# Column copies by byte offset, seven batches per chunk on ScalarE, in halves of 16

## The chip, the cores and the metric

The kernel runs on one core of a Trainium2 chip. The metric is the device time of one execution in microseconds (us). An edge-softmax graph layer is computed in float32; nothing but the time changes with the edit described here.

## The reference

There are 12,500 nodes with 64 features, and 200,000 edges sorted by their target node, each with a source node, a target node and 64 edge features. `h` is the layer-normed and rectified `x`. Then, with two heads:

```
h_edge = ((h[src] + edge_attr) @ W)          # E x 2 heads x 64
s      = leaky(h_edge . attn_l + (h @ W . attn_r)[dst], 0.2)
alpha  = softmax of s over the edges of one target node
ft     = segment_sum(h_edge * alpha, dst);  y = mean over the two heads
out    = x + relu(batchnorm(y))
```

The kernel never forms `h_edge`. It sums `(h[src] + edge_attr) * weight` per node first and multiplies by `W` at the end.

## The kernel before, in words

**Chunks and tiles.** The edges are cut into 49 chunks (`NCH`), a chunk into 16 groups of 256 edges (`CG`, `GROUP`), and a group into two tiles of 128 edges (`EPP`). So a chunk has 32 tiles. Every tile needs the 128 rows `h[src]` of its edges. They come in three ways:

- by default as an indirect DMA of GpSimd, one for each tile (`gather`, line 691, issued on line 698), from the table `h_tab` in DRAM;
- one tile in some chunks (five of eight chunks from chunk 6 on) as 128 small DMAs of SyncE, one for each row (`load_rows`, line 572, `row_tiles`, line 83). The offset of each row is read from the tile `offs` into a register, sixteen at a time (line 459). These offsets are already in bytes;
- the column tiles (`col_tiles`, line 65) as copies inside the on-chip memory. `acc` holds the transposed table (`hT_cols`) in its partitions 96 to 127, and one instruction copies the column of one edge (32 partitions x 2 elements, the two halves of the 64 features) into the buffer `cols`. The column number comes from the tile `coffs` into a register (`col_regs`, line 466). Group 12 is the one treated so: both its tiles in a chunk from chunk 5 on, but only one tile in the chunks whose number leaves 1 when divided by 4 (5, 9, ... 45), and one in the last chunk.

**Who copies the columns.** The 128 columns of a tile are four batches of 32. Batches are dealt in rounds of seven (`COL_BATCHES = (6, 1)`): ScalarE copies six (`load_cols`, line 832), VectorE the seventh (line 1456). The round that is dealt in chunk c starts from batch 7 x (c - 3), so it runs about two chunks ahead of the use. For a batch, an engine reads 32 registers in one load (line 468), then for each column does one fused register instruction that works out the address, and one copy. TensorE adds the copied columns into the transposed edge features (`turn(c, 3)`, line 959) and into the scores (`col_scores`, line 989, which increments `cols_read`); `cols` has room for four tiles.

**The order on ScalarE in a chunk** (`chunk`, line 844):

```
act.wait_ge(open_diff, c + 1)
nc.scalar.activation(fexp[:, :], fdif[:, :], ACT.Exp)      # line 854
act.wait_ge(diff_ok, c + 1)
nc.scalar.activation(pT[:, :], sdif[:, :], ACT.Exp)        # line 858
z_keep_halves(b)                                           # line 829
load_cols(c)                                               # line 863
```

So the two waits of the softmax lie next to each other, and all copies come behind them, before the first wait of the next chunk. VectorE makes `fdif` and, a little later, `sdif` (line 1518). TensorE turns `pT` (line 1064) and increments `p_turned`; VectorE then makes the weighted one-hot tile `scaled`, TensorE forms the sums, VectorE adds them to `acc`.

**What ties GpSimd to the rest** (`keep_step_late`, line 681): from chunk 5 on, the second gather of chunk c waits for the sums of chunk c - 2, and the eighteenth for the turned exponentials of chunk c - 1. Each gather of a buffer also waits until the same buffer has been used two chunks before (`e_ok`).

**Preparation.** `coffs` is worked out once by ten VectorE instructions (lines 1408 to 1417) from `src`, before the first chunk; ScalarE waits for it (`coffs_ok`).

Of the kernel before, what the change touches and what calls it, by code (L numbers as in the profile page):

```python
# [4 lines left out]
N, E, F, H = 12500, 200000, 64, 2  # L5
P = 128
EPP = 2
# [10 lines left out]
NCH = -(-E // CHUNK)  # L18
# [13 lines left out]
NACC = N + WIN  # L32
# [24 lines left out]
COL_G = 12  # L57
COL_FIRST = 5
COL_BUFS = 4
COL_BATCH = 32  # L60
COL_BATCHES = (6, 1)
COL_ROUND = sum(COL_BATCHES)


def col_tiles(c):

    if c < COL_FIRST:
        return []
    return [(j, COL_G) for j in range(1 if c % 4 == 1 or c == NCH - 1 else EPP)]


def cols_upto(c):

    return sum(len(col_tiles(i)) for i in range(c + 1))


def col_batches_upto(c):

    n = cols_upto(c) * P // COL_BATCH
    return n - n // COL_ROUND, n // COL_ROUND  # L80


def row_tiles(c):
# [30 lines left out]
def gnn_kernel(nc, x, src, dst, ea, w_l, gb_l, src_l, src_q, src_c, dst_l, dst_pad, dst_n, dst_r, base_l, base_q, base_o, ea_t, out):  # L114
    f32, i32, u8 = mybir.dt.float32, mybir.dt.int32, mybir.dt.uint8
    ALU, ACT, AX = mybir.AluOpType, mybir.ActivationFunctionType, mybir.AxisListType

    def view(ap, dims, off=0):

        return bass.AP(ap.tensor, ap.offset + off, [list(ap.ap[0])] + [list(d) for d in dims])  # L120

    with ExitStack() as ctx:
        def sb(name, shape, dt=f32):
            return ctx.enter_context(nc.sbuf_tensor(name, shape, dt))
# [11 lines left out]
        acc = sb("acc", [P, H, NACC])  # L136
        accf = acc[:, :, :].rearrange("p h n -> p (h n)")
# [11 lines left out]
        HALF = F // H  # L149
        CP = P - HALF  # L150
# [15 lines left out]
        coffs, coffs_t, coffs_u = (sb(n, [P, EPP * P], i32) for n in ("coffs", "coffs_t", "coffs_u"))  # L166
        row_tile = sb("row_tile", [P, ROW_BUFS, FH])
        cols = sb("cols", [P, COL_BUFS, H, P])
# [37 lines left out]
        cc = sb("cc", [R2, 2, R2])  # L206
# [244 lines left out]
        def tiles_of(c, k):  # L451

            return [(j, g) for g in range(k * GQ, (k + 1) * GQ) for j in range(EPP)
                    if (c * CG + g) * GROUP + j * P < E
                    and (j, g) not in row_tiles(c) + col_tiles(c)]

        def far_regs(c, o0, o1):
# [3 lines left out]
                skip_runtime_bounds_check_because="src and dst hold numbers of nodes")[1]  # L461

        col_batches = [(c, j, r0) for c in range(NCH) for j, g in col_tiles(c) for r0 in range(0, P, COL_BATCH)]
        assert len(col_batches) <= COL_ROUND * (NCH - COL_FIRST)

        def col_regs(c, o0, o1, which):

            return nc.values_load_multi_w_load_instructions(  # L468
                coffs[c:c + 1, o0:o1], engines=[which], min_val=0, max_val=N - 1,
                skip_runtime_bounds_check_because="src and dst hold numbers of nodes")[1]  # L470

        h_bytes = h_tab.rearrange("n f -> (n f)").bitcast(u8)
# [21 lines left out]
        def z_seen(c):  # L494

            return list(range(z_upto(c - 2), z_upto(c - 1)))


        HT = [(i, min(i + 4, NB // EPP)) for i in range(0, NB // EPP, 4)]

        HT_OF = [[n for n, (i, _) in enumerate(HT) if b0 <= i * EPP < b1] for b0, b1 in QS]
        assert all(EPP * HT[n][1] <= b1 for ns, (_, b1) in zip(HT_OF, QS) for n in ns)

        def hT(n):
# [7 lines left out]
        ENG = mybir.EngineType  # L512
# [6 lines left out]
        def _(sp):  # L519
# [72 lines left out]
            for c in range(1, NCH):  # L592
# [6 lines left out]
                if c >= ROW_FIRST - 1:  # L599
                    sp.wait_ge(p_turned, c)  # L600
                    load_rows(c, 1)

            sp.wait_ge(cols_ok, col_batches_upto(NCH - 1)[0])
            sp.wait_ge(cols_dve_ok, col_batches_upto(NCH - 1)[1])
            sp.wait_ge(zT_ok, Z_IN)
            sp.dma_start(zT[F:P, 0:Z_IN, :], view(acc[0:F, 1, :], [[NP_, Z_IN], [1, NP_]])).then_inc(z_packed, 16)
# [22 lines left out]
            for i, (b0, b1) in enumerate(OUT):  # L629
                sp.wait_ge(y_ok, 1 + [t1 for _, t1 in TURN].index(b1))  # L630
                sp.dma_start(y_rows[0:PS[1], b0:b1], xres[0:PS[1], b0:b1]).then_inc(out_in, 16)
# [117 lines left out]
        def _(act):  # L749
# [70 lines left out]
            def z_keep(b, turned, kept):  # L820

                act.wait_ge(turned, b + 1)
                nc.scalar.activation(zT[:, b, :], z_turned(b), ACT.Copy).then_inc(kept, 1)

            def z_keep_halves(b):

                act.wait_ge(zT_made, b + 1)
                for r in range(NR):
                    kept = nc.scalar.activation(acc[0:F, r, b * NP_:(b + 1) * NP_], z_turned(b)[r * F:(r + 1) * F], ACT.Copy)
                kept.then_inc(zT_ok, 1)  # L830

            def load_cols(c):

                b0 = COL_ROUND * (c - COL_FIRST + 2)
                for cc, j, r0 in col_batches[b0:b0 + COL_BATCHES[0]]:
                    n = cols_upto(cc - 1) + j
                    if n >= COL_BUFS:
                        act.wait_ge(cols_read, n - COL_BUFS + 1)
                    for i, r in enumerate(col_regs(cc, j * P + r0, j * P + r0 + COL_BATCH, ENG.Activation), r0):
                        copied = nc.scalar.activation(view(cols[0:HALF, n % COL_BUFS, 0, i:i + 1], [[P, H]]),  # L840
                                                      view(acc[CP:P, 0, bass.ds(r, 1)], [[NACC, H]]), ACT.Copy)
                    copied.then_inc(cols_ok, 1)

            def chunk(c):

                if c == NCH - 1:
                    act.wait_ge(cols_dve_ok, col_batches_upto(c)[1])
                    z_keep(NZ - 5, zT_made, zT_ok)
                if c == NCH - 1:
                    z_keep(NZ - 4, zT_made, zT_ok)  # L850
                act.wait_ge(open_diff, c + 1)
                if c:
                    act.wait_ge(open_all, c)
                nc.scalar.activation(fexp[:, :], fdif[:, :], ACT.Exp).then_inc(open_exp, 1)  # L854
                act.wait_ge(diff_ok, c + 1)
                if c:
                    act.wait_ge(p_turned, c)
                nc.scalar.activation(pT[:, :], sdif[:, :], ACT.Exp).then_inc(p_ok, 1)
                if c < NCH - 1:
                    for b in z_seen(c):  # L860
                        z_keep_halves(b)
                if COL_FIRST - 2 <= c < NCH - 2:
                    load_cols(c)

            def root_table():

# [3 lines left out]
            def closing():  # L870

                chunk(NCH - 1)
                for b in range(NZ - 3, NZ):
                    if b == NZ - 1:
                        root_table()
                        act.wait_ge(last_read, 1)
                    z_keep(b, zT_made, zT_ok)
# [3 lines left out]
            for c in range(NCH - 1):  # L881
                chunk(c)
# [266 lines left out]
        def _(dve):  # L1149
            v = nc.vector  # L1150
            done = [v_steps, 0]

            def step(ins):

                done[1] += 1
                ins.then_inc(done[0], 1)
                dve.wait_ge(done[0], done[1])
# [6 lines left out]
            def signal(s):  # L1164
                dve.sem_inc(s, 1)  # L1165
# [240 lines left out]
            node, t, u = (a[0:NCH, :] for a in (coffs, coffs_t, coffs_u))  # L1406
# [8 lines left out]
            step(v.tensor_scalar(node, node, 1, None, ALU.logical_shift_right))  # L1415
            step(v.scalar_tensor_tensor(t, node, float(NP_), t, ALU.mult, ALU.add))
            step(v.scalar_tensor_tensor(node, u, float(NH), t, ALU.mult, ALU.add))
            signal(coffs_ok)

            def z_block(b, made, read, turned):  # L1420
# [35 lines left out]
            def load_cols(c, i):  # L1456

                if c == COL_FIRST - 2:
                    dve.wait_ge(cols_table_in, 32)
                b0 = COL_ROUND * (c - COL_FIRST + 2) + COL_BATCHES[0] + i  # L1460
                for cc, j, r0 in col_batches[b0:b0 + 1]:
                    n = cols_upto(cc - 1) + j
                    if n >= COL_BUFS:
                        dve.wait_ge(cols_read, n - COL_BUFS + 1)
                    for i, r in enumerate(col_regs(cc, j * P + r0, j * P + r0 + COL_BATCH, ENG.DVE), r0):
                        copied = v.tensor_copy(view(cols[0:HALF, n % COL_BUFS, 0, i:i + 1], [[P, H]]),  # L1466
                                               view(acc[CP:P, 0, bass.ds(r, 1)], [[NACC, H]]))
                    copied.then_inc(cols_dve_ok, 1)

            def chunk(c):  # L1470
# [94 lines left out]
                for i, (g0, g1) in enumerate(sums_of(c)):  # L1565
                    dve.wait_ge(sums_made, 2 * c + i + 1)
                    for g in range(g0, g1):
# [10 lines left out]
                        else:  # L1578
                            added.then_inc(sums_added, 1)
                    if i < COL_BATCHES[1] and COL_FIRST - 2 <= c < NCH - 2:  # L1580
                        load_cols(c, i)
# [165 lines left out]
```

## Time and profile before

| | |
|---|---|
| median of three runs | 3050.21 us (3046.49 to 3059.28) |
| span of the profiled execution, first to last instruction | 1885.4 us |
| the profiled execution's own time beside its span | not given; the median less the span is 1164.8 us |
| POOL (GpSimd) busy | 1389.6 us, 74% |
| DVE (VectorE) busy | 1312.1 us, 70% |
| ACT (ScalarE) busy | 1041.5 us, 55% |
| PE (TensorE) busy | 1042.3 us, 55% |
| DMA engines busy, mean | 83 GB/s moved over the span |

Register, branch and semaphore instructions are not counted as busy, so an engine that mostly loads registers and works out addresses looks idler than it is. An engine's name with a q behind it (ACTq, DVEq, SPq) is its sequencer: the views show register loads (TENSOR_LOAD) and fused register operations (FUSED_REGOPS) under it. "Issue" is time in which an engine waited for nothing that the profile shows. Times in rows are us from the start of the span.

### The profile page before, as it was taken

The numbers are of one execution on the slowest core, as the hardware profiler recorded it, in microseconds if no ns is written. First come the engines' busy times: TensorE is split into PE (matmuls) and PEld (weight loads), VectorE is DVE, ScalarE is ACT, GpSimd is POOL, SyncE is SP. The second block draws the span as 40 slices with busy tenths as digits, with TensorE's granted clock in tenths as the row PEclk, the third lists the DMA queues.
The fourth block names the chain that finished last, engine by engine and source line by source line (L and its number), as shares of the span: only waits on it lengthen the run. The fifth ranks groups of instructions, "written<-read, shape, count | busy, mean of one in ns | idle before, by whom it ended". The sixth has DMA issues, their size and how long they took to land.

```text
span 1885.4 us, 47594 instructions
## 1 busy us (share of the span) xinstructions
PE 1042.3 (55%) x6860; PEld 792.2 (42%) x6860; DVE 1312.1 (70%) x4737; ACT 1041.5 (55%) x8591; POOL 1389.6 (74%) x1477
## 2 busy tenths in 40 slices
PE   2726646556545744655554565545654654564466
PEld 1614534444434533533443353434433543453355
DVE  7878877776676766776766866766766667667676
ACT  2520366666655665666565565665665565566522
POOL 7777677777777777777777777777777777777770
PEclk9857766667666766666666666666666666676667
DMA  8643232232222223222322232232223222222335
GB/s 232 172 107 96 61 89 72 64 95 66 64 84 77 64 64 97 64 64 63 98 64 64 63 98 64 63 97 64 64 63 98 64 63 79 82 64 63 97 72 140
DMA packets 77196, 156.31 MB, mean 83 GB/s; under 512 B 34116, under 2 KB 38736, under 8 KB 70224
## 3 DMA queue, kind: packets, MB, share of 16 engines
q1 hardware_dynamic: 28818, 99.91, 15.9%
q0 software_dynamic: 46944, 49.57, 13.1%
q10 hardware_dynamic: 1112, 3.73, 0.8%
q14 instruction: 266, 2.18, 0.4%
q8 instruction: 56, 0.92, 0.2%
HBM read 141.85 MB, written 9.80 MB: 80 GB/s over the span
## 4 chain that ended last, share of the span: by engine, by line
POOL 59%; issue 21%; PE 7%; DVE 7%; DMA 2%; ACT 2%; ACTq 1%; DVEq 0%; SPq 0%
POOL work L698 58%; PE po L1084 2%; ACT cols L840 1%; PE p_s L985 1%; ACTq L468 1%; PE p_s L947 1%; DMA er_run<-er_tab,er_idx 1%; DMA acc<-in_x 1%; PE pt L972 1%; DMA h_tab<-acc 1%; PE p_s L1014 1%; PE pt L936 1%; DVE work L1215 0%; DVE onehot L1358 0%; POOL er_run L712 0%
## 5 line engine op out<-in xcount | busy, mean ns | idle before, releaser
L698 POOL DMA_INDIRECT work<-h_tab,srcI x1396 | 1319.7, 945 | 430.0 <-issue 423.5
L840 ACT ACTIVATE cols<-acc 32x2 f32 x8352 | 928.3, 201 | 493.8 <-issue 460.6
L1084 PE MATMUL po<-scaled,work 128*65 128x64 f32 x3104 | 297.4, 284 | 60.5 <-issue 57.5
L1084 PEld LDWEIGHTS po<-scaled,work 128*65 128x65 f32 x3104 | 292.0, 200 | 78.0 <-issue 77.1
L1466 DVE COPY cols<-acc 32x2 f32 x1376 | 178.1, 189 | 160.6 <-issue 142.0
L972 PE MATMUL pt<-ident,work 128*128 128x128 f32 x784 | 194.7, 391 | 59.4 <-DVE work L1215 59.3
L1022 PE MATMUL p_s<-ident,elh 128*32 128x128 f32 x196 | 50.6, 411 | 303.9 <-DVE elh L1210 303.9
L1210 DVE COPY elh<-work 128x16 f32<-128x16 f32 (+2 forms) x222 | 40.5, 195 | 227.0 <-DMA work<-h_tab,srcI 225.1
L1570 DVE TENSOR_TENSOR acc<-acc,po 65x64 f32 x776 | 168.4, 217 | 28.0 <-PE po L1084 1.6
L985 PE MATMUL p_s<-work,wpair 128*32 128x256 f32 x784 | 180.5, 384 | 1.6 <-DVEq L1165 1.6
L972 PEld LDWEIGHTS pt<-ident,work 128*128 128x128 f32 x784 | 139.0, 200 | 88.6 <-DVE work L1215 64.2
L1022 PEld LDWEIGHTS p_s<-ident,elh 128*32 128x32 f32 x196 | 25.7, 155 | 315.5 <-DVE elh L1210 311.4
L1061 PE MATMUL p_m<-fexp,ones 1*65 1x2 f32 x98 | 18.4, 255 | 238.5 <-ACT fexp L854 238.5
L1215 DVE TENSOR_TENSOR work<-work,pt 128x512 f32<-128x512 f32 (+2 forms) x222 | 132.7, 607 | 5.9 <-PE pt L972 5.7
L1542 DVE TENSOR_TENSOR scaled<-onehot,p_m 128x2048 f32<-128x2048 f32 x48 | 109.6, 2284 | 19.3 <-PE p_m L1064 18.6
L1061 PEld LDWEIGHTS p_m<-fexp,ones 1*65 1x65 f32 x98 | 14.2, 204 | 257.5 <-ACT fexp L854 257.5
L985 PEld LDWEIGHTS p_s<-work,wpair 128*32 128x32 f32 x784 | 82.9, 111 | 79.3 <-issue 2.5
L1014 PE MATMUL p_s<-ohT_i,er_st 128*32 128x256 f32 x392 | 94.3, 384 | 2.6 <-DVE er_st L1366 2.6
L854 ACT ACTIVATE fexp<-fdif 1x2 f32<-1x2 f32 x49 | 9.9, 203 | 147.3 <-DVEq L1165 146.9
L698 POOL DMA_INDIRECT work<-in_x,srcI x64 | 61.7, 964 | 20.9 <-issue 18.3
L919 PE MATMUL p_q<-wz,acc 65*125 65x65 f32 x376 | 66.4, 332 | 0.0
L1364 DVE TENSOR_TENSOR ohT_i<-ohT_i,p_m 128x1024 f32<-128x1024 int32 x49 | 59.6, 1216 | 6.1 <-DMA ohT_i<-in_dst_n 6.0
(219 smaller groups left out, 1271.0 us busy)
## 6 DMA issues: line engine op xcount, KB each, us to landing
row_tile<-h_tab SPq DMA_DIRECT2D x3392, 0.3 KB
work<-in_ea_t SPq DMA_DIRECT2D x49, 1024.0 KB
ohT_i<-in_dst_n SPq DMA_DIRECT2D x49, 512.0 KB
work<-h_tab,srcI POOLq DMA_INDIRECT x1396
acc<-hT_tab SPq DMA_DIRECT2D x2, 1562.5 KB, 14.4
h_tab<-acc SPq DMA_DIRECT2D x1, 2887.5 KB
work<-in_x SPq DMA_DIRECT2D x1, 2800.0 KB
out<-work SPq DMA_DIRECT2D x5, 448.0 KB
```

The lines of the kernel that those rows point to most:

```text
L698: pool.indirect_dma_start(out=row, out_offset=None, in_=x if c < RAW else h_tab, in_offset=bass.IndirectOffsetOnAxis(ap=srcI[:, c, j, g:g ...
L840: copied = nc.scalar.activation(view(cols[0:HALF, n % COL_BUFS, 0, i:i + 1], [[P, H]]), view(acc[CP:P, 0, bass.ds(r, 1)], [[NACC, H]]), AC ...
L919: m = mm(z_bank(b)[0:NP_, c0:c0 + F1], view(acc[0:F1, hd, 0:1], [[NR, NP_]], b * ZBL + r), wz[:, hd, :], start=True, stop=True)
L972: m = nc.tensor.transpose(pt[n % 2][:, at:at + P], bt[c % 2][:, 2 * k + i, j * P:(j + 1) * P], ident[:, :])
L985: m = mm(sT_ps, wpair[:, i, :, :].rearrange("p h g -> p (h g)"), bt[c % 2][:, i, :], start=(i == 0), stop=False, skip_group_check=True)
L1014: m = mm(sT_ps, er_st[:, b, :, :].rearrange("p h g -> p (h g)"), ohT[:, b, :], start=False, stop=False, skip_group_check=True)
L1022: m = mm(sT_ps[:, j * P:(j + 1) * P], elh[:, c % 2, j, :, :].rearrange("p h g -> p (h g)"), ident[:, :], start=False, stop=True, skip_grou ...
L1084: m = mm(bank[0:F1, w0:w0 + H * WIN], edge[c % 2][:, j, g, :], scaled[:, j * CG + g, :, :].rearrange("p h w -> p (h w)"), start=(j == 0), ...
L1215: added = v.tensor_tensor(edge[q][:, js, g0:g1, 0:F], rows_h[:, :, :, 0:F], turned[:, js, g0 - GQ * k:g1 - GQ * k, :], ALU.add)
L1466: copied = v.tensor_copy(view(cols[0:HALF, n % COL_BUFS, 0, i:i + 1], [[P, H]]), view(acc[CP:P, 0, bass.ds(r, 1)], [[NACC, H]]))
L1542: v.tensor_tensor(scaled[:, :, :, :], view(onehot[:, :, :], [[WIN, CT], [0, H], [1, WIN]]), view(p_m[:, 0:H * CT], [[1, CT], [CT, H], [0, ...
L1570: added = v.tensor_tensor(at, at, bank[0:F1, w0:w0 + H * WIN].rearrange("p (h w) -> p h w", h=H), ALU.add)
```

## The change

Five things are edited. Round size: seven batches for ScalarE and one for VectorE, so eight batches, two tiles, per chunk. Both tiles of group 12 are column tiles in every chunk from 5 on but the last. ScalarE's batches are cut in halves of 16 columns, each with its own register load and its own increment of `cols_ok`. The first half of a chunk stands between the exponential of `fdif` and the wait for `diff_ok`; the other thirteen stand where the copies stood. And `coffs` holds byte offsets (one more multiplication by 4 in the preparation), which index a byte view of `acc` that is then read as float32.

```diff
-COL_BATCHES = (6, 1)
+COL_HALF = COL_BATCH // 2
+COL_BATCHES = (7, 1)

-    return [(j, COL_G) for j in range(1 if c % 4 == 1 or c == NCH - 1 else EPP)]
+    return [(j, COL_G) for j in range(1 if c == NCH - 1 else EPP)]

-    return n - n // COL_ROUND, n // COL_ROUND
+    return 2 * (n - n // COL_ROUND), n // COL_ROUND

+        acc_u8 = accf.bitcast(u8)
+        def col_at(r):
+            r = r.with_bounds(min_val=0, max_val=4 * (N - 1), guaranteed_mod_val=0, out_of_modulus=4)
+            return view(acc_u8[CP:P, bass.ds(r, 4)].bitcast(f32), [[NACC, H]])

-            def load_cols(c):
+            def load_cols(c, first, last):
                 b0 = COL_ROUND * (c - COL_FIRST + 2)
-                for cc, j, r0 in col_batches[b0:b0 + COL_BATCHES[0]]:
+                halves = [(cc, j, r0 + h * COL_HALF) for cc, j, r0 in col_batches[b0:b0 + COL_BATCHES[0]] for h in range(2)]
+                for cc, j, r0 in halves[first:last]:
...
-                    for i, r in enumerate(col_regs(cc, j * P + r0, j * P + r0 + COL_BATCH, ENG.Activation), r0):
-                        copied = nc.scalar.activation(view(cols[0:HALF, n % COL_BUFS, 0, i:i + 1], [[P, H]]),
-                                                      view(acc[CP:P, 0, bass.ds(r, 1)], [[NACC, H]]), ACT.Copy)
+                    for i, r in enumerate(col_regs(cc, j * P + r0, j * P + r0 + COL_HALF, ENG.Activation), r0):
+                        copied = nc.scalar.activation(view(cols[0:HALF, n % COL_BUFS, 0, i:i + 1], [[P, H]]), col_at(r), ACT.Copy)

                 nc.scalar.activation(fexp[:, :], fdif[:, :], ACT.Exp).then_inc(open_exp, 1)
+                if COL_FIRST - 2 <= c < NCH - 2:
+                    load_cols(c, 0, 1)
                 act.wait_ge(diff_ok, c + 1)
...
-                    load_cols(c)
+                    load_cols(c, 1, 2 * COL_BATCHES[0])

             step(v.scalar_tensor_tensor(node, u, float(NH), t, ALU.mult, ALU.add))
+            step(v.tensor_scalar(node, node, 4.0, None, ALU.mult))
             signal(coffs_ok)
...
                         copied = v.tensor_copy(view(cols[0:HALF, n % COL_BUFS, 0, i:i + 1], [[P, H]]),
-                                               view(acc[CP:P, 0, bass.ds(r, 1)], [[NACC, H]]))
+                                               col_at(r))
```

## Rows read from the trace of the kernel before

**Rows 1.** The page, the chain that ended last, by engine.
```profile
POOL 59%; issue 21%; PE 7%; DVE 7%; DMA 2%; ACT 2%; ACTq 1%; DVEq 0%; SPq 0%
```
**Rows 2.** The page, costliest groups: count, busy, mean ns, idle before and what ended it.
```profile
L698 POOL DMA_INDIRECT work<-h_tab,srcI x1396 | 1319.7, 945 | 430.0 <-issue 423.5
L840 ACT ACTIVATE cols<-acc 32x2 f32 x8352 | 928.3, 201 | 493.8 <-issue 460.6
```
**Rows 3.** Line L698 by stretch: length, busy (x count), granted TensorE clock, DMA share, GB/s.
```profile
1200.00:1400.00 200.00, 151.11 (x160) 0.66 0.25 70
```
**Rows 4.** Timeline of ACT, chunk 22: start, us, what, how many, idle before.
```profile
899.15 0.20 ACT L854 ACTIVATE fexp<-fdif 1x2 f32<-1x2 f32 x1 [3.45 <-DVEq L1165]
901.26 0.41 ACT L858 ACTIVATE pT<-sdif 32x256 f32<-32x256 f32 x1 [1.91 <-DVE sdif L1518]
...
909.16 3.51 ACT L840 ACTIVATE cols<-acc 32x2 f32 x32 [1.97 <-issue]
914.64 0.74 ACT L840 ACTIVATE cols<-acc 32x2 f32 x6 [1.97 <-issue]
915.55 2.87 ACT L840 ACTIVATE cols<-acc 32x2 f32 x26 [0.18 <-issue]
920.39 3.51 ACT L840 ACTIVATE cols<-acc 32x2 f32 x32 [1.97 <-PE p_s L993]
...
931.62 3.51 ACT L840 ACTIVATE cols<-acc 32x2 f32 x32 [1.97 <-issue]
935.15 0.20 ACT L854 ACTIVATE fexp<-fdif 1x2 f32<-1x2 f32 x1
```
**Rows 5.** Timeline of ACT: the first exponential of chunks 3, 6 and 46.
```profile
208.16 0.20 ACT L854 ACTIVATE fexp<-fdif 1x2 f32<-1x2 f32 x1 [22.71 <-DVEq L1165]
...
312.06 0.20 ACT L854 ACTIVATE fexp<-fdif 1x2 f32<-1x2 f32 x1 [0.94 <-DVEq L1165]
...
1789.13 0.20 ACT L854 ACTIVATE fexp<-fdif 1x2 f32<-1x2 f32 x1 [5.03 <-DVEq L1165]
```
**Rows 6.** Waits: who waited for whom, us in total, times, longest.
```profile
PE p_s L1022 <- DVE elh L1210: 303.9, 45, 10.4
```
**Rows 7.** Register loads of 32, by source line: count, ns minimum/median/maximum, first and last start.
```profile
L468 ACTq TENSOR_LOAD <-coffs x261: 1948/1977/2169, 210.3 to 1802.4; - x131
L468 DVEq TENSOR_LOAD <-coffs x43: 2323/2376/2434, 220.7 to 1771.7; - x43
```
**Rows 8.** Register loads: L459 loads sixteen, L430 four to sixteen, L481 one.
```profile
L459 SPq TENSOR_LOAD <-offs x212: 1133/1234/1410, 219.0 to 1771.2; - x106
L430 DVEq TENSOR_LOAD <-lanes x145: 343/571/1107, 132.2 to 1827.3; - x145
L481 DVEq TENSOR_LOAD <-flag x1: 314/314/314, 1810.0 to 1810.0; - x1
L481 ACTq TENSOR_LOAD <-flag x1: 466/466/466, 1826.4 to 1826.4; - x1
L481 SPq TENSOR_LOAD <-flag x1: 442/442/442, 1861.8 to 1861.8; - x1
```
**Rows 9.** Fused register operations by source line.
```profile
L840 ACTq FUSED_REGOPS  x8352: 46/46/57, 212.5 to 1807.8; - x199
L1466 DVEq FUSED_REGOPS  x1376: 57/57/71, 223.1 to 1778.3; - x197
L1570 DVEq FUSED_REGOPS  x733: 46/46/53, 146.5 to 1861.4; - x184
L481 ACTq FUSED_REGOPS  x1: 179/179/179, 1826.9 to 1826.9; - x1
```
**Rows 10.** Timeline of ACT: a short activation with another right behind it.
```profile
43.54 0.21 ACT L764 ACTIVATE acc<-acc 125x24 f32<-125x24 f32 x1
43.65 1.48 ACT L778 ACTIVATE acc<-acc 125x1536 f32<-125x1536 f32 x1
```
**Rows 11.** One of the ten steps that prepare `coffs`, by source line.
```profile
L1411 DVE TENSOR_SCALAR coffs_u<-coffs x1: 319/319/319, 128.0 to 128.0; 49x256 int32<-49x256 int32 x1
```

More of the change, by code:

```diff
@@ L464, in gnn_kernel @@
         assert len(col_batches) <= COL_ROUND * (NCH - COL_FIRST)
+        acc_u8 = accf.bitcast(u8)
+        def col_at(r):
+            r = r.with_bounds(min_val=0, max_val=4 * (N - 1), guaranteed_mod_val=0, out_of_modulus=4)
+            return view(acc_u8[CP:P, bass.ds(r, 4)].bitcast(f32), [[NACC, H]])
         def col_regs(c, o0, o1, which):
             return nc.values_load_multi_w_load_instructions(
-                coffs[c:c + 1, o0:o1], engines=[which], min_val=0, max_val=N - 1,
+                coffs[c:c + 1, o0:o1], engines=[which], min_val=0, max_val=4 * (N - 1),
                 skip_runtime_bounds_check_because="src and dst hold numbers of nodes")[1]
```

## The prediction

> **What bounds the kernel now.** The first view to read is the chain of waits [rows 1]: 59% of the span is GpSimd's work and 21% is "issue". The page's groups [rows 2] say whose issue that is: 1396 indirect gathers of 945 ns, and before them 430.0 us idle of which 423.5 is GpSimd's own issue. Cut into a stretch [rows 3], 160 gathers fit in 200 us, so a gather costs 1.25 us, 0.945 busy and 0.30 between, with nothing left over. GpSimd paces the steady part, and a gather less is worth 1.25 us as long as nobody else is slower.
>
> The reader should look next at who comes second. ACT is 55% busy by the page, but its copies have 460.6 us of "issue" in front of them [rows 2]. The timeline of a chunk [rows 4] shows what it is: a 1.97 us pause before every 32 copies, which is the load of 32 registers [rows 7]. In chunk 22, ACT starts `pT` at 901.26 and the next `fexp` at 935.15, directly behind its last copy: 33.9 us without waiting for anybody that matters. Chunk 6 begins with only 0.94 us of waiting [rows 5]. So ACT needs about 33.7 us for a chunk, with a few tenths more for the two exponentials, while GpSimd takes, over the chunks from 6 on, 29.6 gathers (32 tiles less 1.75 column tiles less 5/8 row tile) x 1.25 = 37.0 us. ACT has about 3.2 us of slack in a chunk, hidden in a busy share that looks low. TensorE waits 303.9 us in 45 chunks for the last gathered quarter [rows 6], 6.8 us per chunk, so TensorE and VectorE have more room than ACT has.
>
> **The change part by part.** *GpSimd.* Chunks 5, 9, ... 45 gather one tile less: 11 x 1.25 = 13.75 us less on the engine that paces. Its need falls to 29.4 x 1.25 = 36.7 us per chunk. This is all that the change can give: nothing else is taken off GpSimd.
>
> *ACT, the seventh batch.* Two batches take 909.16 to 920.39, or 11.23 us, one 5.6 [rows 4]. Six make 33.7, seven 39.3 us.
>
> *ACT, the address.* In a run of 32 copies one costs (3.51 - 0.20) / 31 = 0.107 us [rows 4], and 46 ns of that is the fused register operation [rows 9]. Before, the address of a column is three steps: add the place of partition 96, times 4, add the base. For line 1570, in partitions from 0, it is two: times 4, add the base. On VectorE the first costs 57 ns and the second 46 [rows 9]: 11 ns for a step. ACT's three take 46, so I scale by 46/57 and get 9 ns for the multiplication that byte offsets make superfluous. I expect two additions to remain, not one, and a copy of 0.098 us. Bounds: nothing saved, 0.107; and 0.095, which the engine itself seems to need, since an activation of 24 elements is followed by the next 0.11 us later [rows 10] and the copies have 22 elements less. Seven batches have 224 copies: 224 x 0.009 = 2.0 us less, between 0 and 2.7.
>
> A rule of the Trainium skill (ScalarE: Activation LUTs, section What ACT_TABLE_LOAD costs) speaks on the lower bound: an activation with immediate scale and bias takes 186 ns plus 0.833 ns per element, and back-to-back ones overlap by about 93 ns. For two elements that is 188 - 93 = 95 ns, and by it alone the copies could go down to an estimated 0.095 us and no further. The copies here are recorded with 201 ns [rows 2], not 188, and with the same overlap 201 - 93 would be the 0.107 that they have already; the rule then says that the saving is nil, which is the third rival below.
>
> *ACT, the halves.* Seven loads of 32 become fourteen of 16. The trace has no load of 16 on ACT. From below: VectorE's longest load on line 430 is that of sixteen, 1107 ns, against its 2376 for 32 [rows 7, 8]; the same ratio of ACT's 1977 gives 0.92 us. From above: SyncE's loads of sixteen have a median of 1.234 us, and its load of one takes 442 ns against ACT's 466 [rows 8], so the two are alike there; a straight line from ACT's 466 for one to 1977 for 32 gives 1.19. In between: from one register to 16 VectorE adds 793 ns and SyncE 792, and from one to 32 VectorE adds 2062 where ACT adds 1511; 793 x 1511 / 2062 on top of 466 gives 1.05, and I take that. Fourteen are 14.7 us against 13.8 now, 0.9 more, between -0.9 and +3.4.
>
> *Sum on ACT.* 39.3 - 2.0 + 0.9 = 38.2 us per chunk. That is above GpSimd's 36.7, so ACT becomes the pace, and the gathers that are left out are hidden.
>
> *The first half between the waits.* Now ACT idles 2.11 us from `fexp` to `pT` when it has arrived early [rows 4]. The half needs 1.05 + 16 x 0.098 = 2.6 us, so `pT`, and behind it TensorE's turn and VectorE's `scaled`, come 0.5 us later than they could in such chunks; the 6.8 us of slack cover that. It makes the idle time useful, so it is not an extra cost, and it is in the sum. Once ACT is late, `sdif` is ready before ACT gets there, and the place of the half saves nothing.
>
> *Waits and queues.* The halves are dealt exactly two chunks ahead, into the buffers of the chunk whose `cols_read` TensorE signals before that chunk's scores are finished. So no half waits for a buffer; the wait shown at 920.39 in [rows 4] goes. Behind a late ACT stand `fexp` (VectorE's correction of the open node) and `pT`; GpSimd's eighteenth gather waits for the latter by its step, so GpSimd slows down with ACT.
>
> *Small parts.* The added step on `coffs` costs about 0.32 us once [rows 11], on VectorE's path before the first chunk: I count 0.3, and 0 to 0.5 as bounds. VectorE's one batch gets 32 x 11 ns = 0.35 us shorter per chunk, covered. TensorE gets eleven column tiles more, about 1 us each, in its idle time.
>
> *Sum for the kernel.* `fexp` starts at 208.16 in chunk 3, where the copies begin, and at 1789.13 in chunk 46 [rows 5]: 1581 us for 43 chunks, 36.8 each. After: 43 x 38.2 = 1643. That is +62 us on the span of 1885.4, giving about 1947. What lies around the span is 3050.2 - 1885.4 = 1164.8 us by the median of the runs shown, as no time of the profiled execution itself is given; no instruction runs in it, and I leave it as it is. So 3050 + 62 = 3112 us.
>
> **Rivals.** *GpSimd stays the pace* (not slower). If ACT's chunk stays under about 36.7 us, the eleven gathers come off in full: 3050 - 13.75 + 0.3 = 3037 us. The point is sharp: it needs a load of sixteen at 0.94 us with the copy at 0.098, or at 0.99 with the copy at 0.095. The ratio on VectorE (0.92) is for it, SyncE's sixteen at 1.13 us even at its quickest against it. If the two engines come out equal, the time is 3040 to 3060. *The loads are like SyncE's.* At 1.19 us the chunk takes 40.2 us, 148 us more: 3198. The forecast with one term at its upper bound. *The copies do not get faster.* If the activation, and not its register work, sets the 0.107 us, the chunk takes 40.2 too and the time is again near 3198. Against it: the 24-element case of [rows 10] shows room. *The byte view costs more than it saves.* The view is cut in bytes and then read as float32. If a division by 4 and the multiplication both stay in the address, the register work grows. The fused operation of line 481, comparisons and a logical step, takes 179 ns where three plain steps take 46 [rows 9], so a step of a costlier kind is worth some 40 ns: 224 x 0.05 = 11 us per chunk, near 3550 us.
>
> **How the numbers follow.** ACT becomes the pace in some measure, at the forecast's terms (37.1 to 39.5 us per chunk): 0.42. GpSimd stays the pace, or the two come out equal: 0.37. Loads like SyncE's: 0.09. Copies not faster: 0.07. Costlier address: 0.05. 0.5%, or 15 us, is about what a measurement of this kernel can tell from no change. The largest gain is 0.45% by the sum, so "faster" needs the rival at its full gain and a little more from the measurement: 0.13. "Same" takes the rest of that rival and a small part of the forecast's low end, 0.31. "Slower": 0.56. The range goes from the full gain, 3034, to the loads or copies at their bound, 3198. The forecast's own range is 3065 to 3168.
>
> **What would show it.** Right: ACT's fused operation at about 37 ns and copies 0.098 us apart; ACT's load of sixteen near 1.05 us; about 38 us from one `fexp` to the next, the last copy directly followed by `fexp` in every chunk; idle time of GpSimd before its gathers that ends with TensorE's `p_m`, none of which is there now; ACT and ACTq at the head of the chain instead of POOL. The prediction is wrong if GpSimd's gathers still follow each other every 1.25 us over the whole middle, or if the `fexp` of a chunk still waits for VectorE, or if time outside the span moves.

## The result, and the profile after

| | ratio to before | median | before beside it |
|---|---|---|---|
| forecast | 1.020 | 3112 us (3034 to 3198) | 3050.21 us |
| measured | 1.0543 [1.0518, 1.0569] | 3217.06 us | 3051.63 us |
| measured again on another chip (f1 below) | 1.0106 [1.0090, 1.0123] | 1908.87 us | 1889.12 us |

The direction was right and the size was not: 3217 us lies outside the range. The profiled execution took 3223.36 us beside a span of 3221.6, so 1.8 us lie around a span, not 1164.8 (in all executions on record that list both, 1.7 to 2.9 us). The kernel before, profiled again (e1), took 3116.16 us with a span of 3114.4. The span of 1885.4 us and the median of 3050.21 us, which the forecast joined, were therefore of two conditions of the hardware. Below, a *smooth* chip is one on which the kernel before takes about 1889 us (two chips), a *stepping* chip one on which it takes 3050 to 3110 (two more, and where the measurement above was made). Every ratio is against the kernel before on the same chip.

The page of the changed kernel at 3223.36 us: the span, the chain that ended last, and the groups that answer to [rows 2].

```profile
span 3221.6 us, 50893 instructions
...
ACTq 32%; ACT 31%; issue 27%; PE 3%; DVE 2%; another core or an unknown queue 1%; DMA 0%; DVEq 0%; SPq 0%
...
L706 POOL DMA_INDIRECT work<-h_tab,srcI x1385 | 1308.2, 945 | 1762.3 <-PE p_m L1074 1097.6
L849 ACT ACTIVATE cols<-acc 32x2 f32 x9760 | 1133.9, 191 | 1702.8 <-issue 1666.1
```

A gather still takes 945 ns [rows 2], and there are eleven fewer, but GpSimd's idle time before them has grown from 430.0 to 1762.3 us, and 1097.6 of it ends with TensorE's turn of `pT`. ScalarE's copies are short, and between them lie 1666.1 us of "issue" (460.6 before). Its timeline in the same trace shows what that is (start, us, what, how many, idle before).

```profile
1507.47 1.62 ACT L849 ACTIVATE cols<-acc 32x2 f32 x16 [0.98 <-issue]
1509.11 0.20 ACT L862 ACTIVATE fexp<-fdif 1x2 f32<-1x2 f32 x1
...
1521.53 0.20 ACT L849 ACTIVATE cols<-acc 32x2 f32 x1 [0.53 <-issue]
1522.23 0.20 ACT L849 ACTIVATE cols<-acc 32x2 f32 x1 [0.49 <-issue]
1522.96 0.20 ACT L849 ACTIVATE cols<-acc 32x2 f32 x1 [0.53 <-issue]
1524.32 0.20 ACT L849 ACTIVATE cols<-acc 32x2 f32 x1 [1.16 <-issue]
...
1554.60 0.20 ACT L849 ACTIVATE cols<-acc 32x2 f32 x1 [1.19 <-issue]
1555.99 0.20 ACT L849 ACTIVATE cols<-acc 32x2 f32 x1 [1.20 <-issue]
1557.18 1.62 ACT L849 ACTIVATE cols<-acc 32x2 f32 x16 [0.98 <-remote]
1559.77 1.62 ACT L849 ACTIVATE cols<-acc 32x2 f32 x16 [0.98 <-issue]
```

Sixteen copies take 1.62 us at 1507 and at 1557. Between, single copies start 0.7 or 1.4 us apart. The same chunk of GpSimd's timeline:

```profile
1512.95 0.95 POOL L706 DMA_INDIRECT work<-h_tab,srcI  x1 [25.84 <-PE p_m L1074]
...
1527.94 0.94 POOL L706 DMA_INDIRECT work<-h_tab,srcI  x1 [0.30 <-issue]
1533.38 0.95 POOL L706 DMA_INDIRECT work<-h_tab,srcI  x1 [4.50 <-PE po L1094]
...
1552.12 0.94 POOL L706 DMA_INDIRECT work<-h_tab,srcI  x1 [0.31 <-issue]
```

The steps begin some 5 us after a run of gathers begins (1518) and end some 4 us after its last gather (1532, 1556). GpSimd itself keeps its 1.25 us. Cutting the chunk there gives, for ScalarE's copies (length, busy and count, granted clock, DMA share, GB/s):

```profile
1500.00:1518.00 18.00, 11.03 (x107) 0.50 0.30 97
1518.00:1532.00 14.00, 3.15 (x16) 0.62 0.15 24
1532.00:1539.00 7.00, 3.74 (x34) 0.60 0.14 22
1539.00:1556.00 17.00, 2.65 (x14) 0.66 0.16 26
1556.00:1566.00 10.00, 5.90 (x57) 0.50 0.01 1
```

The 31 us of the two stepping stretches hold 30 copies, which take under 4 us elsewhere. The busiest DMA stretch is the first, 97 GB/s, and it has no steps; the granted clock is not lower in them (0.62 and 0.66) than beside them. So neither the bytes moved nor the granted clock goes along with the steps here; the gathers do. With the edges drawn where address and DMA-issuing instructions last over 0.4 us, I count 87 such stretches, 1566 us of the 3222; the kernel before has 86, 1524 of 3114 us, in its own stepping run, and none in the trace that the prediction read. So the other engines' streams of short instructions do most of their work between the runs of gathers and not beside them.

### The profile page after: what moved, and what is told of

It reads as the page before. It is cut to its first block, busy times and chain, and to the rows that moved or that the text cites. A ratio compares the mean times of both kernels' runs of the same rounds, so it can differ in the third digit from the quotient of the medians.

```text
span 3221.6 us, 50893 instructions
## 1 busy us (share of the span) xinstructions
PE 1216.5 (38%) x6948; PEld 894.2 (28%) x6948; DVE 1320.5 (41%) x4728; ACT 1248.0 (39%) x9999; POOL 1378.0 (43%) x1466
## 4 chain that ended last, share of the span: by engine, by line
ACTq 32%; ACT 31%; issue 27%; PE 3%; DVE 2%; another core or an unknown queue 1%; DMA 0%; DVEq 0%; SPq 0%
ACT cols L849 31%; ACTq L849 20%; ACTq L476 13%; PE po L1094 1%; ACT acc L837 1%; PE p_s L995 0%; DMA h_tab<-acc 0%; PE p_s L1024 0%; PE po L1016 0%; PE pt L982 0%; DVE acc L1581 0%; DVE work L1225 0%; PE pt L1153 0%; DMA er_run<-er_tab,er_idx 0%
## 5 line engine op out<-in xcount | busy, mean ns | idle before, releaser
L706 POOL DMA_INDIRECT work<-h_tab,srcI x1385 | 1308.2, 945 | 1762.3 <-PE p_m L1074 1097.6
L849 ACT ACTIVATE cols<-acc 32x2 f32 x9760 | 1133.9, 191 | 1702.8 <-issue 1666.1
L1094 PE MATMUL po<-scaled,work 128*65 128x64 f32 x3104 | 384.3, 302 | 516.6 <-issue 513.1
L1094 PEld LDWEIGHTS po<-scaled,work 128*65 128x65 f32 x3104 | 350.3, 217 | 560.5 <-issue 557.3
L1477 DVE COPY cols<-acc 32x2 f32 x1376 | 190.9, 191 | 604.2 <-issue 603.6
L995 PE MATMUL p_s<-work,wpair 128*32 128x256 f32 x784 | 237.1, 467 | 7.1 <-issue 4.4
L929 PE MATMUL p_q<-wz,acc 65*125 65x65 f32 x376 | 79.1, 307 | 250.8 <-issue 250.8
L995 PEld LDWEIGHTS p_s<-work,wpair 128*32 128x32 f32 x784 | 100.6, 135 | 124.9 <-issue 73.3
L929 PEld LDWEIGHTS p_q<-wz,acc 65*125 65x125 f32 x376 | 70.8, 243 | 210.5 <-issue 210.1
L1074 PE MATMUL p_m<-ident,pT 32*128 32x32 f32 x98 | 20.5, 300 | 126.7 <-ACT pT L868 121.3
```

Of the source, the lines that this page charges most:

```text
L706: pool.indirect_dma_start(out=row, out_offset=None, in_=x if c < RAW else h_tab, in_offset=bass.IndirectOffsetOnAxis(ap=srcI[:, c, j, g:g ...
L929: m = mm(z_bank(b)[0:NP_, c0:c0 + F1], view(acc[0:F1, hd, 0:1], [[NR, NP_]], b * ZBL + r), wz[:, hd, :], start=True, stop=True)
L995: m = mm(sT_ps, wpair[:, i, :, :].rearrange("p h g -> p (h g)"), bt[c % 2][:, i, :], start=(i == 0), stop=False, skip_group_check=True)
L1094: m = mm(bank[0:F1, w0:w0 + H * WIN], edge[c % 2][:, j, g, :], scaled[:, j * CG + g, :, :].rearrange("p h w -> p (h w)"), start=(j == 0), ...
```

## The experiments

**What the parts do on a stepping chip.** Four kernels on one chip, the kernel before beside them at 3109 us. e1 is the kernel before, unchanged. 

> The kernel before, unchanged. In the trace of the changed kernel, in stretches of 13 to 41 us in every chunk, register operations and small DMAs take 0.7 us each on ScalarE and SyncE, while GpSimd keeps its 1.25 us per gather. The profile of before shows none of it and spans 1885.4 us, against a median of 3050. Stall theory: the slow stretches belong to the ordinary executions of both kernels, the profile of before was an exception, and this run spans about 3050 us with such stretches in every chunk. Work theory (the changed kernel is slower because ScalarE has more to do in a chunk): the slow stretches are new, this run's trace has none, and its span is near 1885.

Measured: 1.0003 [0.9985, 1.0020]. Its page, chain:

```profile
SPq 31%; issue 26%; another core or an unknown queue 15%; DVE 14%; DVEq 4%; PE 4%; DMA 3%; ACT 2%; ACTq 2%
```

The stall theory holds: the span is 3114.4 us, with steps in every chunk from 3 to 46. [Rows 1] had GpSimd at the head with 59%. Here it isn't in the chain, and SyncE's stream for the row tiles heads it. ScalarE is not idle beside it either. The waits of `fexp` for VectorE (us, times), of this run and then of the trace that the prediction read:

```profile
  DVEq L1165: 79.7, 14
```
```profile
  DVEq L1165: 173.2, 35
```

Of the 43 chunks between `fexp` of 3 and of 46, 32 end with `fexp` directly behind the last copy (within 0.5 us); in the other trace 14 do. So on a stepping chip the kernel before already has ScalarE without slack in three chunks of four. A forecast for this condition could not be read from the trace of before.

e2 is before with byte offsets alone (six whole batches). 

> The kernel before with byte offsets alone: six whole batches, all behind the second exponential. ScalarE's register operation becomes one addition and a copy follows the last after 0.094 us instead of 0.107, with the same number of instructions. Work theory: ScalarE was not the pace, so the same time, 3050 within 10 us. Stall theory, if the stalls come from how fast ScalarE issues: slower by 1 to 4%; if they come from the count of instructions: the same.

```diff
-                view(acc[CP:P, 0, bass.ds(r, 1)], [[NACC, H]])
+                col_at(r)
...
```

Measured: 0.9785 [0.9761, 0.9810]; the chunk (from `fexp` of 3 to `fexp` of 46, over 43) fell from 63.33 to 61.96 us. The byte offsets are a gain here, which neither theory had allowed. A chunk is 1.37 us shorter, where six batches have 192 copies that are each 0.012 us quicker, 2.3 us; `fexp` is directly behind the last copy in 30 of the 43 chunks. That the gain comes through these chunks fits, but was not tested by itself.

e3 is the change with seven whole batches, all behind `pT`. 

> The changed kernel with whole batches of 32, all seven behind the second exponential: seven register loads in a chunk instead of fourteen, nothing between the waits. Work theory: a chunk is 0.2 us shorter for the loads, but the waits idle 2 us again where ScalarE is early, so within 1% of the changed kernel's 3217. Stall theory: as the changed kernel within 1%, unless the place of the first half matters.

```diff
-COL_HALF = COL_BATCH // 2
+COL_HALF = COL_BATCH
...
-                    load_cols(c, 0, 1)
...
```

Measured: 1.0433 [1.0412, 1.0454], 66.50 us per chunk: 4.5 us more than e2, and the chain has ACTq 32%, ACT 32%, where e2's has SPq 41%. The seventh batch makes ScalarE the pace in every chunk (`fexp` is directly behind the last copy in all 43) and costs 6.6% here (1.0433 / 0.9785), more than the whole loss of the change. Against the changed kernel's 1.0543 it is 1.0% faster, at the edge of the 1% that was expected; the kernel before stood at 3109 us beside the one and at 3052 beside the other.

e4 is the change with six batches, in halves, the first half between the waits. 

> The changed kernel with six batches in twelve halves and the column tiles as before (one in every fourth chunk). Work theory: ScalarE has 5.2 us less to do in a chunk than in the changed kernel, so it is not the pace and the time is that of before, 3050 within 15 us. Stall theory with stalls in proportion to the column copies: also near before, 3050 to 3090. If halves or byte offsets cause the loss: near 3217.

```diff
-COL_BATCHES = (7, 1)
+COL_BATCHES = (6, 1)
```

(and `c % 4 == 1` back in `col_tiles`.) Measured: 0.9915 [0.9882, 0.9947], 62.74 us per chunk. Beside e2, on the same chip, the halves with their first one between the waits cost 1.3% (0.9915 / 0.9785). e4 takes 22.6 us less than the kernel before, a little outside the 15 us expected, and is far from the 3217 that would have put the loss on halves or byte offsets.

**Who is behind the steps, first try.** The next two sets of runs fell on smooth chips, so e5, e6 and e7 answered another question, and their figures for the stepping case could not be tried on them. e5 is before without SyncE's row tiles (`ROW_SHARE` 0 in place of 5), e6 before without column tiles (`COL_FIRST = NCH`), e7 both; the tiles go to GpSimd's gathers.

> The kernel before without its row tiles (all but the last chunk's): 26 tiles more are gathered by GpSimd, 3328 small DMAs of SyncE fall away. Alternation theory: while GpSimd gathers, the other engines' instruction streams crawl, so a chunk lasts about its gathers plus the longest stream that is left for the time between; that stream is SyncE's in the kernel before. Then SyncE's goes, GpSimd gains 26 x 1.25 = 33 us, and ScalarE's stream comes next: 2 to 6% faster. Overlap theory (engines run side by side, the slowest paces): GpSimd is not the pace in these runs, SyncE is, so about the same gain. If the small DMAs cause the stalls: no stretches of 0.7 us steps are left, and the time falls below 2200 us.

> The kernel before without column tiles: 87 tiles more are gathered, ScalarE and VectorE copy no columns. Overlap theory: SyncE stays the pace, no change within 2%. Alternation theory: 109 us more of gathers, and SyncE's stream stays, so 2 to 4% slower. If ScalarE's fast stream of short instructions causes the stalls: no slow stretches, and below 2200 us.

> Neither row tiles nor column tiles: GpSimd gathers every tile, 113 more, 40 us a chunk. Alternation theory: hardly any work is left for the time between, so a chunk lasts 40 to 50 us and the kernel 2150 to 2600 us, far faster than before although GpSimd has 141 us more to do. Overlap theory: GpSimd paces at 40 us a chunk, near 2050. If the stalls are a matter of the count of instructions alone, they are gone as well.

Measured: 1.0163 [1.0146, 1.0180], 1.0483 [1.0465, 1.0500] and 1.0652 [1.0634, 1.0670]. In time +30, +92 and +123 us for 26, 87 and 113 gathers more, which by 1.25 us each are 33, 109 and 141. On a smooth chip GpSimd is the pace, as [rows 1] and [rows 3] say, and what is taken from the others buys nothing.

e8 is the change with all fourteen halves behind `pT`. 

> The changed kernel with all fourteen halves behind the second exponential. Against whole batches (1.0433 of before) and the changed kernel (1.054): if the fourteen register loads cost the 1%, this is at 1.055 to 1.065; if the place of the first half cost it, at 1.045.

```diff
-                if COL_FIRST - 2 <= c < NCH - 2:
-                    load_cols(c, 0, 1)
                 act.wait_ge(diff_ok, c + 1)
...
-                    load_cols(c, 1, 2 * COL_BATCHES[0])
+                    load_cols(c, 0, 2 * COL_BATCHES[0])
```

Measured: 1.0109 [1.0092, 1.0126], against 1.0106 with the half between the waits (f1). Its place is worth nothing once ScalarE is late, on a smooth chip; the figures expected were those of a stepping chip, where this was not run.

**The forecast's own condition.** f1 is the changed kernel itself on a smooth chip, f2 is e2, f3 is e3.

> The changed kernel, unchanged, to see it beside the kernel before on another chip. So far the kernel before took 3050 and 3110 us where the traces show the 0.7 us steps, and 1888 us where they do not. Two-condition theory: the ratio depends on which condition the chip is in. Without the steps ScalarE's chunk is 14 x 2.60 us (a load of 1.027, sixteen copies 0.094 apart) and about 1 us of fetch gaps, 37.5 us against the 36.7 of GpSimd: 1.5 to 2.5% slower than before, at 1915 to 1935. With the steps again 5 to 6% slower.

> Byte offsets alone again (0.9785 of before with the steps). Without the steps GpSimd paces and ScalarE only gets more slack: the same within 0.3%. With the steps: 2% faster.

> Seven whole batches behind the second exponential again (1.0433 of before with the steps). Without the steps the seven loads are 7 x 0.08 us less than fourteen halves, but the 2.1 us between the two exponentials stay idle when ScalarE is early: 37.1 us a chunk, near the 36.7 of GpSimd, so 0 to 1% slower than before. With the steps 4% slower.

f1 measured 1.0106 [1.0090, 1.0123]. Its page (chain) and its timeline of ACT over one chunk:

```profile
span 1907.3 us, 50893 instructions
...
ACT 43%; ACTq 24%; PE 13%; issue 10%; DVE 5%; POOL 2%; DMA 2%; DVEq 0%; SPq 0%
```
```profile
917.38 0.20 ACT L862 ACTIVATE fexp<-fdif 1x2 f32<-1x2 f32 x1
918.42 1.62 ACT L849 ACTIVATE cols<-acc 32x2 f32 x16 [0.84 <-issue]
920.07 0.41 ACT L868 ACTIVATE pT<-sdif 32x256 f32<-32x256 f32 x1
920.51 0.55 ACT L837 ACTIVATE acc<-p_q 64x125 f32<-64x125 f32 x2
...
926.66 1.62 ACT L849 ACTIVATE cols<-acc 32x2 f32 x16 [0.98 <-issue]
929.27 1.62 ACT L849 ACTIVATE cols<-acc 32x2 f32 x16 [0.99 <-issue]
...
953.88 1.24 ACT L849 ACTIVATE cols<-acc 32x2 f32 x12 [0.17 <-issue]
955.14 0.20 ACT L862 ACTIVATE fexp<-fdif 1x2 f32<-1x2 f32 x1
```

`fexp` follows the last copy 0.21 us after that copy's start in this chunk, and 0.35 us at most in the 43: ScalarE waits for nobody and is the pace. The first `fexp` stands at 206.87, that of chunk 46 at 1814.88, 37.40 us per chunk (36.8 before, [rows 5]). The chunk is the 37.5 us expected, the loss of 1.06% is less than the 1.5 to 2.5% expected. By source line (count, ns minimum/median/maximum), first the copies' address and the copies, then the loads of 16:

```profile
L849 ACTq ALU_OP  x9760: 35/35/48, 208.1 to 1836.1; - x200
L849 ACT ACTIVATE cols<-acc x9760: 187/188/206, 208.2 to 1836.2; 32x2 f32 x200
...
L476 ACTq TENSOR_LOAD <-coffs x610: 1007/1029/1222, 206.9 to 1833.6; - x153
```

f2 measured 0.9998 [0.9988, 1.0008]: the quicker copies alone are covered by GpSimd. f3 measured 0.9957 [0.9940, 0.9973], 8.7 us less, of the 13.75 that eleven gathers are worth, where 0 to 1% slower was expected. Its page (chain) and its loads:

```profile
POOL 59%; issue 22%; DVE 7%; PE 6%; DMA 3%; ACT 3%; DVEq 1%; ACTq 0%; SPq 0%
```
```profile
L476 ACTq TENSOR_LOAD <-coffs x305: 1950/1982/2168, 208.1 to 1795.6; - x153
```

GpSimd heads the chain again. From one `fexp` to the next are 36.60 us, beside 29.4 gathers x 1.25 = 36.7. Over the middle its gathers wait for nobody; ScalarE has no wait before `fexp` either, here as in all 43 chunks:

```profile
970.08 1.24 ACT L849 ACTIVATE cols<-acc 32x2 f32 x12 [0.18 <-issue]
973.26 3.12 ACT L849 ACTIVATE cols<-acc 32x2 f32 x32 [1.95 <-issue]
976.41 0.20 ACT L862 ACTIVATE fexp<-fdif 1x2 f32<-1x2 f32 x1
976.52 0.40 ACT L866 ACTIVATE pT<-sdif 32x256 f32<-32x256 f32 x1
```

So the two engines come out equal. A whole batch takes 1.95 + 3.12 = 5.07 us, a split one 2 x (0.98 + 1.62) = 5.20; the 0.13 us, seven times a chunk, is the 0.8 us between 36.60 and 37.40. e8 (1.0109) and f3 differ in the split alone, so the split, not the seventh batch, lost the gain on a smooth chip. e7's kernel, run once more beside these, stood at 1.0649 [1.0631, 1.0666].

**Who is behind the steps, second try.** The last four runs met a stepping chip (before 3051.9 us). g1 is the change with the first batch alone in halves.

> Seven batches per chunk by byte offsets; only the first is copied in two halves, the first of them between ScalarE's two waits, the second and six whole batches behind pT's exponential. Theory (a half costs ScalarE a load of 1.01 us for 16 registers and a batch of 32 one of 1.98, so each batch kept whole saves about 0.1 us; and the half between the waits stands in idle time only where ScalarE is not late): without the 0.7 us steps GpSimd keeps the pace at 36.6 us per chunk, as in the version with seven whole batches, and the ratio is 0.995 to 0.999. Rival (the first half between the waits makes pT late and with it everything behind it): 36.9 to 37.2 per chunk, 1.003 to 1.010. If the chip shows the steps: 1.03 to 1.05, between all halves (1.054) and all whole (1.043).

```diff
+                whole = [(cc, j, r0, COL_BATCH) for cc, j, r0 in col_batches[b0:b0 + COL_BATCHES[0]]]
+                halves = [(cc, j, r0 + h * COL_HALF, COL_HALF) for cc, j, r0, _ in whole[:1] for h in range(2)] + whole[1:]
...
```

Measured: 1.0463 [1.0442, 1.0484], 65.40 us per chunk. The ratio is between all halves (1.0543) and all whole (1.0433), as expected, and its interval overlaps that of all whole, which was measured on another chip. Whether it would gain on a smooth chip was not seen.

> The kernel before with neither the column tiles of ScalarE and VectorE nor SyncE's row tiles: all 113 tiles go to GpSimd's gathers. Where the kernel before takes about 1890 us this stood at 1.065. The open question is what the 0.7 us steps are, where the kernel before takes about 3050 to 3110. Theory (the steps hold up the instruction streams of the other engines while GpSimd gathers, and the gathers themselves keep 1.25 us): with no long stream left on ScalarE and SyncE there is little to hold up, the chunk is its 28 to 32 gathers and a short rest, and the time is 2000 to 2300 us, a ratio of 0.65 to 0.75. Rival (the condition makes the gathers or all engines slower by a factor): the ratio stays at 1.0 to 1.07. If the steps are absent it is 1.065 again.

> The kernel before without column tiles (no copies by ScalarE and VectorE, 87 more gathers), SyncE's row tiles kept. Without the steps 1.048 as before. With them: theory (each engine's stream of short instructions is held up beside the gathers, whatever the others do) leaves SyncE's stream of 128 register loads and small DMAs per row tile as the pace, a ratio of 0.95 to 1.05; rival (ScalarE's copies are what brings the steps about) takes the steps away and gives 0.63 to 0.68.

> The kernel before without SyncE's row tiles (26 more gathers, 3328 small DMAs less), the column copies kept. Without the steps 1.016 as before. With them: theory (each engine's own stream is held up) leaves ScalarE's copies as the pace, 0.90 to 1.02; rival (SyncE's small DMAs beside the gathers' transfers bring the steps about) takes them away and gives 0.60 to 0.65.

g2 (e7's kernel) measured 0.7823 [0.7777, 0.7868], g3 (e6's) 0.9217 [0.9197, 0.9237], g4 (e5's) 0.9846 [0.9825, 0.9867]. The rival that either stream brings the steps about falls: neither kernel came near 0.6, and both traces still have the steps. A MOVE of SyncE (29 ns in the median) lasts up to 1402 ns in g3, an address operation of ScalarE (46 ns) up to 1396 ns in g4. The rival to g2, that all engines are slower by one factor, falls too, since that kernel gained. With both gone 21.8% is won where 6.5% is lost on a smooth chip. In g3 SyncE heads the chain (SPq 40%), in g4 ScalarE is back in it (ACTq 21%, ACT 17%): each stream is held up for itself. Two of the figures that I set were missed, 0.65 to 0.75 for g2, which won less, and 0.95 to 1.05 for g3, which won more. Why g2 stays above 0.75 shows in the score matmuls by source line, of g2 and of the same kernel on a smooth chip:

```profile
L985 PE MATMUL p_s<-work,wpair x784: 376/379/636, 90.9 to 2322.8; 128*32 128x256 f32 x196
its engine sat idle before it (us, times) until:
  issue: 277.9, 400
```
```profile
L985 PE MATMUL p_s<-work,wpair x784: 379/379/634, 71.3 to 1961.0; 128*32 128x256 f32 x196
its engine sat idle before it (us, times) until:
...
  issue: 2.7, 11
```

The matmuls last the same, but before 400 of them TensorE's stream is late. TensorE's stream is held up with no column copy of ScalarE and only the last chunk's row tile of SyncE in the program; what is left is the gathers. That the gathers bring the steps about is argued from this and from the timing above; no kernel without gathers was run. A chunk of g2 takes 46.55 us, 40 of them gathers.

## Why the prediction was right or wrong

**What failed** is one step: "What lies around the span is 3050.2 - 1885.4 = 1164.8 us ... no instruction runs in it, and I leave it as it is." A gap of 38% between a span and its median was the strongest signal on the page, and I carried it as a constant although no row said what it was. It was time inside the instruction streams: e1 spans 3114.4 of its 3116.16 us. The text named "time outside the span moves" as what would refute it, but gave that no rival and no price.

With it fell the overlap on which the sum stood, that ScalarE works beside the gathers and has 3.2 us of slack: on the stepping chip it has none in 32 of 43 chunks (e1). That the direction came out right there is in part luck.

**In its place**, the sum on a stepping chip. ScalarE needs 37.4 us for its work (f1). The stretches of steps take 35.6 us of a chunk, and the 49 copies and two loads that they let through are worth 6.7. 37.4 + 35.6 - 6.7 = 66.3 us; measured 66.05. This is bookkeeping on the same trace, not a second test. GpSimd's side of the chunk, from what ended the idle time before its gathers in the same trace (us, times), gives the same:

```profile
its engine sat idle before it (us, times) until:
  PE p_m L1074: 1097.6, 44
  issue: 417.4, 1353
  PE po L1094: 258.5, 46
```

29.4 gathers of 1.25 us are 36.7; the eighteenth waits 24.9 us for `pT`, which lies behind the copies, and the second 5.6 for the sums. Less the two 0.3 us already in the 1.25, that is 66.6. ScalarE's stream is thus for the most part added to GpSimd's gathers, not hidden beside them, so the seventh batch costs nearly its full length: e3 less e2, 4.5 us per chunk, of the 5.07 that it takes in f3. Against that the byte offsets save 2.2%; the halves cost 1.3% (e4 beside e2).

**What held**, on the smooth chips of which the rows were, by its terms:

- *GpSimd is the pace, 1.25 us a gather* [rows 1, 3]: right; e5 to e7 give 1.05 to 1.17 us per gather added, somewhat less than the 1.25.
- *ScalarE is second, with 3.2 us of slack, and overtakes*: right. Chunk 37.40 us, forecast 38.2 with 37.1 to 39.5; the chain went from POOL to ACT and ACTq; `fexp` behind the last copy in each chunk.
- *Copy 0.098 us*: 16 copies take 1.62, so (1.62 - 0.20) / 15 = 0.095. 224 x (0.107 - 0.095) = 2.7 us, not 2.0. The address operation is an ALU_OP of 35 ns where there was a fused one of 46 [rows 9]; 37 was forecast, with two additions left, and no row shows how many steps either holds. The activation itself went from 201 to 188 ns. The spacing is the lower bound that I had read off [rows 10]. The Trainium skill (ScalarE: Activation LUTs, section What ACT_TABLE_LOAD costs) puts an activation with immediate scale and bias at 186 ns plus 0.833 per element with 93 ns of overlap, 95 ns for two elements; this trace agrees with it, and my use of it for the rival "the saving is nil" does not hold.
- *Load of sixteen 1.05 us*: 1.029; fourteen cost 14 x 1.029 - 7 x 1.977 = 0.6 us more, not 0.9. Scaling VectorE's and SyncE's common rise [rows 7, 8] by ScalarE's own slope was the right estimate, and the plain ratio (0.92) and the straight line (1.19) were both off. The straight line is 1.20 when worked out, not 1.19.
- *Place of the first half worth nothing once ScalarE is late*: right, e8.
- *The upper end of the range*: the loads' own upper bound, SyncE's 1.234 us, stands in the text as +3.4 us, yet 3198 was worked out with 1.19. With the bound the chunk is 40.7 us and the range ends at 3219. That would have held 3217, by luck alone, for no load of sixteen took that long in the median (1.03). The costlier address is 3594 by its own 11 us on the forecast, not "near 3550".
- *GpSimd's idle time that ends with `p_m`, "none of which is there now"*: the trace of before has 4.6 us of it, twice; f1 has 45.8 us, 32 times.
- *+62 us*: +19.8, from 43 x (37.40 - 36.77) = 27 in the chunks less some 5 in what comes before and behind them (span +21.9). On the measured terms ScalarE's chunk is 39.3 - 2.7 + 0.6 = 37.2. The error of 0.8 us per chunk is small beside 38.2 but is more than half of the 1.4 us by which 38.2 exceeded the pace of 36.8. [Rows 5] with f1's and f3's chunks show how close the engines were: 36.8, 37.4, 36.6. There, a term of 0.01 us times 224 copies decides the size, and one of 0.1 us times seven loads the sign: f3, whose loads are whole, gains.

## What to carry to other kernels

Before any engine's row is read, the profiled span must be set against the times: if they differ by more than a few us (1.7 to 2.9 here), the profile is of another condition, and the forecast needs the second condition as a case with its own price, or at least a range for it. Where one engine paces and another is 10% behind, cost the second one's added stream per instruction, register loads included; splitting a load of 32 registers in two costs little, but seven times a chunk it was the whole gain. A stream of hundreds of tiny instructions that is free beside one engine's DMAs in one condition is paid nearly in full in the other (4.5 of 5.07 us): gathers alone were 6.5% slower in one and 21.8% faster in the other, and of the kernels run in both only the byte offsets (0.9998 and 0.9785) were no loss in either.

## What the hardware showed that I had not expected

- On a stepping chip, in stretches that begin some 5 us after a run of gathers 1.25 us apart and end some 4 us after its last, the instruction streams of ScalarE, SyncE, VectorE and TensorE advance in steps of 0.7 or 1.4 us. An address operation of 35 ns (median) lasts up to 1382 ns there, against 48 at most on a smooth chip. The copies, the matmuls and the gathers themselves last the same. What makes a chip do so is open: no kernel here turned it off, and none without gathers was tried. Every execution on record has its span recorded, so it isn't shown either whether the recording takes part.
- The address of a dynamic column: by element a fused operation of 46 ns, by byte an ALU_OP of 35 ns; and an activation with the byte address is 188 ns, not 201.
- A register load on ScalarE: 466 ns for one [rows 8], 1029 for sixteen, 1982 for 32. It is not a straight line from one to 32, which would give 1.20 us for sixteen.
- The engine at the head of the chain need not be the only one without slack. SyncE heads it in e1 and e2 (SPq 31% and 41%), and yet `fexp` stands directly behind ScalarE's last copy in 32 and 30 of 43 chunks, and quicker copies gained 2.2%. How the two share a chunk was not taken apart.
